# Running the shared expert's half units beside the routing in the second expert stage

## The chip, the cores and the metric

The kernel runs on one core of one Trainium2 chip. Its time is the device time of one execution in microseconds (us); where several executions were timed, their median is given. TensorE (PE) multiplies matrices, VectorE (DVE) does elementwise work and reductions, ScalarE (ACT) the table functions, GpSimd (POOL) elementwise work beside them, and SyncE (SP) issues the DMAs. Each engine works off its own queue in order and waits on semaphores.

## The reference

Two blocks, each a gated cross-attention and a gated mixture of experts, over x of 4 x 256 x 256. The change concerns the second mixture of experts (all tokens, 64 routed experts of width 64, four per token, and two shared experts of width 256):

```python
xm = x.mean(axis=1)
h1 = gelu(xm @ te_W1.T + te_b1)
task_dist = softmax(h1 @ te_W2.T + te_b2)                 # dataset head
dom = task_dist @ affinity.T                              # one row per batch
logits = (flat @ Wr.T).reshape(b, t, E) + 0.5 * dom[:, None, :]
scores = softmax(logits)
_, topk_idx = top_k(logits + router_bias, K)              # K = 4
topk_scores = scores[topk_idx] / (sum + 1e-8)
combine = zeros(n, E); combine[topk_idx] += topk_scores   # the shares
h = silu(flat @ Wg[e]) * (flat @ Wu[e])                   # for every expert
out = sum_e (h * combine[:, e]) @ Wd[e]
out = out + sum_i (silu(flat @ Sg[i]) * (flat @ Su[i])) @ Sd[i]   # shared
```

The shared experts take no shares: they need the tokens alone. flat is the layernorm of x, 1024 tokens.

## The kernel before

The program has four stages in one order: attention, experts, attention, experts. Between them the tokens are normalized and turned (`act_turn`, `pe_turn`, `norm`), so that xnT holds them with features on the partitions.

In an expert stage the work is cut into units of 128 hidden columns: in the second stage four units of the shared experts (128 columns each) and then 32 pairs of routed experts. A unit is done in two half units of 512 tokens each. A half unit is `pe_up` (L377: six matmuls for the gate into bank 4, six for the up product into bank 5), ScalarE's silu and VectorE's product (`act_ffn` L319, `ffn` L1545), and `pe_down` (L394: six matmuls, added into banks 0 to 3, which `pe_zero` L368 has cleared by four matmuls with zeros). All products are of split numbers: a high and a low part, three matmuls for one. ScalarE copies the high part of the hidden values (L333), VectorE subtracts it for the low one (L1561). POOL splits the weights of a unit (`split_weights` L667: L674, L675 for gate and up, L679, L680 for down) and makes the low part of the tokens (`stream_rest` L662). TensorE's order is up of half unit j+1, then down of half unit j. Weights and shares have two slots each. For a routed half unit VectorE first multiplies the silu with the experts' shares (L1553), which SP has broadcast to the partitions (wB) from a scratch tensor (w1s) in DRAM.

The second expert stage runs in this order before:

- SP (from L531): router constants, `shared` weights 0 to 3, then `store_shares` (waits for the turned shares, stores them, waits for the landing), then `pair1` for the routed pairs, which loads weights and broadcasts shares.
- TensorE (L1164 to L1211): the turn; the dataset head (two products, one small transpose); then, for each of eight token tiles, two products with the router's weights and one with the affinities; eight transposes of the shares; `pe_zero`; then the half units.
- VectorE (L1687 to L1728): mean of the tokens, the softmax of the dataset head, `shifted` (copy of the logits, maximum, subtract), exp on ScalarE, bias, four largest of 64 (max and match-replace over eight tiles), normalizing, `keep_shares` (L1540), and then `ffn` for the eight half units of the shared experts, and the loop over routed pairs.
- ScalarE (L858 to L868): gelu and exp of the dataset head, exp of the router, then silu and copies of the half units.

So the shared half units stand behind the whole routing in all queues.

Of the kernel before, what the change touches and what calls it, by code (L numbers as in the profile page):

```python
# [31 lines left out]
P = 128  # L32
# [121 lines left out]
def program(nc, a, out, stages=4):  # L154

    ctx = ExitStack()
    with ctx:
# [3 lines left out]
        def sb(name, shape, dt=F32, scope=ctx):  # L161
# [131 lines left out]
            "logits_made r_shifted r_exp sel_ready pos_made w_ready w_turned wT_ready "  # L293
# [25 lines left out]
        def act_ffn(act, u0, i, units, q0):  # L319

            for j in range(units):
# [131 lines left out]
        def _(sp):  # L453
# [138 lines left out]
            def pair1(e, slot, split, free):  # L592
# [3 lines left out]
                for j in range(2):  # L596
# [3 lines left out]
                    sp.dma_start(wd[n, slot, :], a["L1_ffn_Wd"][e * 2 + j]).then_inc(w, 16)  # L600
                w = s.bslot1 if slot else s.bslot0
# [4 lines left out]
            for j in range(2 * NSH):  # L606
                shared(j, j % 2, None if j < 2 else U0 + j - 1)
            store_shares(w1s, E1, 2)
            for r in range(2):
                pair1(r, r, U0 + 2 * NSH + r - 1, 2 * U0)  # L610
            with sp.Fori(1, E1 // 4) as i:
                for slot in range(2):
                    pair1(i * 2 + slot, slot, i * 2 + (U0 + 2 * NSH + slot - 1), i * 4 + (2 * U0 + 2 * slot - 2))
# [5 lines left out]
        def _(pool):  # L619
# [42 lines left out]
            def stream_rest(k):  # L662

                pool.wait_ge(s.xT_hi, KD * k)
                g_.tensor_tensor(xT[:, 1], xnT[:], xT[:, 0].bitcast(F32), ALU.subtract).then_inc(s.xT_lo, 1)
# [55 lines left out]
        def _(act):  # L721
# [67 lines left out]
            with act.Fori(0, U0 // 2) as i:  # L789
                act_ffn(act, 0, i, 4, 0)  # L790
# [71 lines left out]
            nc.scalar.activation(td[:, 1, :], td[:, 0, :], ACT.Exp).then_inc(s.tl_exp, 1)  # L862
            act.wait_ge(s.r_shifted, 2)
            nc.scalar.activation(re[:], rl[:, :, 0:E1], ACT.Exp).then_inc(s.r_exp, 1)
            u0 = 2 * U0
            act_ffn(act, u0, None, 8, None)
            with act.Fori(0, E1 // 4) as i:
                act_ffn(act, u0 + 8, i, 4, u0)  # L868
# [3 lines left out]
        def _(pe):  # L872
# [165 lines left out]
            pe.wait_ge(s.xT_lo, 1)  # L1038
# [127 lines left out]
            pe.wait_ge(s.router_loaded, 16 * 16)  # L1166
            pe.wait_ge(s.xm_ready, 1)
# [5 lines left out]
            pe.wait_ge(s.td_ready, 1)  # L1173
            nc.tensor.transpose(ps[0:ND, 6, 0:B], td[:, 3, :], ident[0:B, 0:B]).then_inc(s.td_turned, 1)
            pe.wait_ge(s.tdT_ready, 1)
            for t in range(NT):
                for k in range(KD):
                    nc.tensor.matmul(ps[:, 7, t * E1:(t + 1) * E1], xnT[:, k, t * P:(t + 1) * P], wr1[:, k, :],
                                     start=k == 0, stop=False)
                ins = nc.tensor.matmul(ps[:, 7, t * E1:(t + 1) * E1], tdT[:, t // TB, :], aff1[:], start=False, stop=True)  # L1180
            ins.then_inc(s.logits_made, 1)
            pe.wait_ge(s.w_ready, 2)
            for t in range(NT):
                ins = nc.tensor.transpose(ps[0:E1, 4 + t // 4, (t % 4) * P:(t % 4 + 1) * P], rw[:, t, :], ident[:])
            ins.then_inc(s.w_turned, 1)
            pe.wait_ge(s.wT_ready, 2)
# [3 lines left out]
            pe.wait_ge(s.xT_lo, 2)  # L1190
            pe_up(pe, u0, None, 0, U0 + 1)
            for j in range(8):
                if j < 7:
                    pe_up(pe, u0, None, j + 1, U0 + (j + 1) // 2 + 1)
                else:
                    pe_up(pe, u0 + 8, None, 0, first + 1)
                pe_down(pe, u0, None, j, U0 + j // 2 + 1)
            last = E1 // 4 - 1
# [17 lines left out]
        def _(dve):  # L1216
# [323 lines left out]
            def keep_shares(E, k):  # L1540

                dve.wait_ge(s.w_turned, k)
                v.tensor_copy(wtf[0:E, :], ps[0:E, 4:6, :].rearrange("p a n -> p (a n)")).then_inc(s.wT_ready, 1)

            def ffn(u0, i, units, q0):  # L1545
                for j in range(units):
# [40 lines left out]
            keep_shares(E0, 1)  # L1587
# [204 lines left out]
```

## Time and profile before

| what | value |
|---|---|
| median of three runs | 2046.72 us (2046.35 to 2048.01) |
| profiled execution, its own time | 2044.75 us |
| its span in the profile | 2043.0 us |
| TensorE busy | 1876.8 us (92%) |
| VectorE busy | 1173.6 us (57%) |
| ScalarE busy | 1037.8 us (51%) |
| POOL busy | 321.4 us (16%) |
| DMA | 96.56 MB, mean 47 GB/s |

The span is the time between the first and the last instruction that the profiler saw; the 1.75 us between it and the execution's own time lie around it. TensorE's share is an average over four stages, so a change within one stage is read there: by the stretches of that stage, by the chain of waits (which work ended last and released the next) and by the timeline of each engine. A busy TensorE is not one at its peak: the granted clock has two levels, 1.2 and 2.4 GHz, shown as 0.50 and 1.00.

### The profile page before, as it was taken

Reading aid. Unit: us, or ns where it says so; the run is one execution under the profiler, and the core shown is the slowest. Engines: PE = TensorE matmul, PEld = TensorE weight load, DVE = VectorE, ACT = ScalarE, POOL = GpSimd, SP = SyncE. Lnnn points to the kernel's source line nnn. Section 1 sums busy time; section 2 is a strip of 40 time slices with the busy share of each in tenths; the row PEclk is TensorE's granted clock in tenths of the full one; section 3 lists DMA queues with packets and bytes.
Section 4 is the critical chain, followed back from the end, with each engine's and each line's share of the span. In section 5 each row is a group of like instructions: output and inputs, shape, how many; then the busy total and the mean of one; then the engine's idle time right before and its main releaser. Section 6 shows DMA issues by size and latency. Waiting matters only on the chain.

```text
span 2043.0 us, 29167 instructions
## 1 busy us (share of the span) xinstructions
PE 1876.8 (92%) x8775; PEld 1281.9 (63%) x8775; DVE 1173.6 (57%) x1893; ACT 1037.8 (51%) x1703; POOL 321.4 (16%) x292
## 2 busy tenths in 40 slices
PE   5889898859997999999999999999999994999998
PEld 3444444548886666666666666666666663888886
DVE  8565746246666665546654476544665445566665
ACT  2576677613333565556655565555655551222222
POOL 3010101024441100000000000000000002444452
PEclk8899999969998999999999999999999995999999
DMA  2422404064441110000100001000000001255453
GB/s 90 101 59 59 99 19 101 1 215 109 108 114 40 33 33 0 0 0 1 33 0 0 0 1 33 0 0 0 0 1 0 0 0 36 73 116 112 108 115 78
DMA packets 110124, 96.56 MB, mean 47 GB/s; under 512 B 72836, under 2 KB 94472, under 8 KB 109416
## 3 DMA queue, kind: packets, MB, share of 16 engines
q1 hardware_dynamic: 110056, 95.67, 18.8%
q8 instruction: 41, 0.67, 0.1%
q14 instruction: 27, 0.22, 0.0%
HBM read 73.73 MB, written 1.44 MB: 37 GB/s over the span
## 4 chain that ended last, share of the span: by engine, by line
PE 81%; DVE 10%; ACT 2%; SPq 2%; POOL 2%; issue 2%; DMA 1%; ACTq 0%; DVEq 0%; POOLq 0%
PE ps L1137 18%; PE ps L1074 17%; PE ps L390 16%; PE ps L401 8%; PE ps L954 4%; PE ps L941 4%; PE ps L1151 3%; PE ps L1085 2%; PE ps L888 2%; DVE s_rk L1631 2%; SPq L491 2%; POOL s_stage L705 1%; PE ps L1109 1%; PE ps L1146 1%; DVE s_rq L1627 1%
## 5 line engine op out<-in xcount | busy, mean ns | idle before, releaser
L852 ACT ACTIVATE s_p<-ps,s_g,s_rk 128x256 f32<-128x256 f32 (+1 forms) x832 | 416.7, 560 | 298.5 <-PE ps L1074 268.5
L1074 PE MATMUL ps<-s_qq,s_ctxT 128*128 (+2 forms) x1248 | 498.9, 513 | 2.7 <-ACT s_ksq L826 2.7
L1137 PE MATMUL ps<-s_p,s_ctx 128*128 128x512 f32 (+1 forms) x832 | 416.7, 595 | 12.8 <-ACT s_p L852 12.8
L1663 DVE TENSOR_TENSOR s_dsum<-s_dsum,s_p 128x512 f32<-128x512 f32 (+1 forms) x384 | 265.8, 692 | 234.0 <-ACT s_p L852 222.3
L1074 PEld LDWEIGHTS ps<-s_qq,s_ctxT 128*128 128x128 f32 (+1 forms) x1248 | 231.3, 186 | 200.0 <-issue 163.3
L390 PE MATMUL ps<-s_xT,s_wgus 128*128 128x512 f32 x1440 | 350.4, 393 | 3.8 <-DVE s_hw L1559 3.5
L390 PEld LDWEIGHTS ps<-s_xT,s_wgus 128*128 128x128 f32 x1440 | 272.6, 189 | 62.4 <-DVE s_hw L1559 3.9
L770 ACT ACTIVATE s_p<-ps,s_bsm 128x1024 f32<-128x1024 f32 x208 | 219.3, 1110 | 93.1 <-PE ps L954 82.9
L1137 PEld LDWEIGHTS ps<-s_p,s_ctx 128*128 128x128 f32 (+1 forms) x832 | 156.9, 189 | 76.8 <-ACT s_p L852 24.6
L1561 DVE TENSOR_TENSOR s_hs<-s_hw,s_hs 128x512 fp32r<-128x512 f32 x120 | 141.3, 1177 | 82.5 <-ACT s_hs L333 82.5
L401 PE MATMUL ps<-s_hs,s_wds 128*128 128x512 f32 x720 | 183.9, 391 | 1.8 <-DVE s_hs L1561 1.8
L333 ACT CAST s_hs<-s_hw 128x512 fp32r<-128x512 f32 x120 | 74.5, 621 | 196.0 <-DVE s_hw L1559 196.0
L941 PE MATMUL ps<-s_qz,s_kT 96*128 96x512 f32 x416 | 155.6, 473 | 16.6 <-ACT s_p L770 8.6
L1074 PE MATMUL ps<-s_wk,s_ctxT 128*128 128x512 f32 (+1 forms) x624 | 167.8, 413 | 2.4 <-ACT s_ksq L826 2.2
L401 PEld LDWEIGHTS ps<-s_hs,s_wds 128*128 128x128 f32 x720 | 135.0, 189 | 31.7 <-DVE s_hs L1561 2.7
L705 POOL TENSOR_TENSOR s_stage<-s_stage,s_rq 128x2048 f32<-128x2048 f32 x8 | 28.9, 3611 | 784.5 <-DVE s_rq L1635 784.5
L826 ACT ACTIVATE s_ksq<-ps 128x512 f32<-128x512 f32 (+1 forms) x208 | 117.7, 607 | 67.5 <-PE ps L1074 39.2
L1631 DVE TENSOR_REDUCE s_rk<-s_ksq 128x4 f32<-128x512 f32 (+1 forms) x208 | 130.9, 676 | 33.6 <-ACT s_ksq L826 33.1
L329 ACT ACTIVATE s_sg<-ps 128x512 f32<-128x512 f32 x120 | 71.8, 598 | 132.1 <-PE ps L390 131.9
L1074 PEld LDWEIGHTS ps<-s_wk,s_ctxT 128*128 128x128 f32 (+1 forms) x624 | 111.1, 184 | 38.9 <-issue 9.8
L1553 DVE TENSOR_TENSOR s_hh<-s_sg,s_wB 128x512 f32<-128x512 f32 x112 | 77.4, 691 | 92.8 <-ACT s_sg L329 82.5
L941 PEld LDWEIGHTS ps<-s_qz,s_kT 96*128 96x128 f32 x416 | 70.2, 194 | 83.0 <-issue 55.1
(240 smaller groups left out, 1837.2 us busy)
## 6 DMA issues: line engine op xcount, KB each, us to landing
s_wB<-w1s SPq DMA_DIRECT2D x64, 256.0 KB, 3.9
s_kT<-s_kst SPq DMA_DIRECT2D x96, 128.0 KB, 2.3
s_kT<-s_kst SPq DMA_DIRECT2D x96, 80.0 KB, 2.1
s_wB<-w0s SPq DMA_DIRECT2D x16, 384.0 KB, 3.7
s_wB<-w0s SPq DMA_DIRECT2D x16, 256.0 KB, 4.1
s_wgu<-in_L_ffn_Wg_dram SPq DMA_DIRECT2D x64, 64.0 KB, 2.8
s_wgu<-in_L_ffn_Wu_dram SPq DMA_DIRECT2D x64, 64.0 KB, 2.6
s_wd<-in_L_ffn_Wd_dram SPq DMA_DIRECT2D x64, 64.0 KB, 2.5
```

Of the source, the lines that this page charges most:

```text
L390: ins = nc.tensor.matmul(ps[:, 4 + g, :], wgus[:, slot, w, g, k, :], xT[:, x_, k, n], start=c == 0, stop=c == len(ops) - 1)
L401: ins = nc.tensor.matmul(ps[:, 2 * half + k, :], wds[:, slot, w, k * P:(k + 1) * P], hs[:, j % 2, h, :], start=False, stop=False, skip_gro ...
L770: nc.scalar.activation(p0[:, n % 4, :], ps[:, 2 * (n % 3):2 * (n % 3) + 2, :].rearrange("p a n -> p (a n)"), ACT.Exp, bias=bsm[:, col:col ...
L826: nc.scalar.activation(ksq1[0:r, n % KSQ, :], ps[0:r, n % 4, :], ACT.Square).then_inc(s.k1_squared, 1)
L852: ins = nc.scalar.activation(p1[0:r, BANK1[t], j, :], ps[0:r, BANK1[t], j * SQ:(j + 1) * SQ], ACT.Exp, bias=g1[0:r, 3:4], scale=rk_col(t, ...
L941: ins = nc.tensor.matmul(ps[:, 2 * (n % 3) + i, :], kT0[0:32 * COPIES, g, i, t * P:(t + 1) * P], qz[0:32 * COPIES, g % 2, i, :], start=Tru ...
L954: ins = nc.tensor.matmul(ps[32 * h:32 * h + 32, SUMBANK, dca * SQ:dca * SQ + SQ], vg[:, b % 2, t + dca, c:c + 2 * D0], p0[:, n % 4, h * SQ ...
L1074: ins = nc.tensor.matmul(out, lhs(x_), rhs(y_), start=first and n == 0, stop=last and n == 2)
L1137: nc.tensor.matmul(ps[:, 4, :], ctx1[0:ROWS1[t], t, :], p1[0:ROWS1[t], BANK1[t], :, :].rearrange("p a n -> p (a n)"), start=t == 0, stop=t ...
L1561: v.tensor_tensor(hs[:, j % 2, 1, :], hw[:, j % 2, :], hs[:, j % 2, 0, :].bitcast(F32), ALU.subtract).then_inc(s.hs_lo, 1)
L1631: v.tensor_reduce(rk1[0:r, u, 4 * q:4 * q + 4], ksq1[0:r, n % KSQ, :].rearrange("p (h d) -> p h d", h=4), AX, ALU.add).then_inc(s.k1_reduc ...
L1663: v.tensor_tensor(dsum[0:r, :], dsum[0:r, :], pt[0:r, :], ALU.add).then_inc(s.summed, 1)
```

## The change

- TensorE multiplies the tokens with the router's weights right behind the turn, into bank 7, without the affinity part. The dataset head follows, then the zeroing and the shared half units. The transpose of the dataset distribution stands behind up(1), four products with the affinities (one per batch, into bank 6) behind down(0), and the transposes of the shares (into banks 6 and 7, no longer 4 and 5) behind down(4).
- VectorE adds the affinities to its copy of the logits in an instruction of its own. Its routing work is put between the half units 0 to 5 of the shared experts.
- ScalarE does silu and copies of half units 0 to 2, then the router's exp, then 3 to 7.
- POOL makes the low part of the tokens in two instructions, one for each half of the tokens (in the first expert stage as well, since both use the same function). TensorE waits for the first half before up(0), and for the second before up(1).
- SP loads the weights of the first two routed pairs ahead of the store of the shares. `pair1` is split into `pair1` (weights) and `shares1` (broadcasts).

The diff, without the lines that only pass a range where a count stood, or a bank number:

```diff
-            def pair1(e, slot, split, free):
+            def pair1(e, slot, split):
 
                 sp.wait_ge(s.wd_split, split)
...
+
+            def shares1(e, slot, free):
...
                 w = s.bslot1 if slot else s.bslot0
                 sp.wait_ge(s.h1_made, primed(free))
                 for j in range(2):
@@ -605,12 +608,15 @@
 
...
             for j in range(2 * NSH):
                 shared(j, j % 2, None if j < 2 else U0 + j - 1)
+            for r in range(2):
+                pair1(r, r, U0 + 2 * NSH + r - 1)
             store_shares(w1s, E1, 2)
             for r in range(2):
-                pair1(r, r, U0 + 2 * NSH + r - 1, 2 * U0)
+                shares1(r, r, 2 * U0)
             with sp.Fori(1, E1 // 4) as i:
                 for slot in range(2):
-                    pair1(i * 2 + slot, slot, i * 2 + (U0 + 2 * NSH + slot - 1), i * 4 + (2 * U0 + 2 * slot - 2))
+                    pair1(i * 2 + slot, slot, i * 2 + (U0 + 2 * NSH + slot - 1))
+                    shares1(i * 2 + slot, slot, i * 4 + (2 * U0 + 2 * slot - 2))
 
             store(sp)
...
             def stream_rest(k):
 
                 pool.wait_ge(s.xT_hi, KD * k)
-                g_.tensor_tensor(xT[:, 1], xnT[:], xT[:, 0].bitcast(F32), ALU.subtract).then_inc(s.xT_lo, 1)
+                for half in range(2):
+                    n = slice(half * HALF, (half + 1) * HALF)
+                    g_.tensor_tensor(xT[:, 1, :, n], xnT[:, :, n], xT[:, 0, :, n].bitcast(F32), ALU.subtract).then_inc(s.xT_lo, 1)
...
             nc.scalar.activation(td[:, 1, :], td[:, 0, :], ACT.Exp).then_inc(s.tl_exp, 1)
+            u0 = 2 * U0
+            act_ffn(act, u0, None, range(3), None)
             act.wait_ge(s.r_shifted, 2)
             nc.scalar.activation(re[:], rl[:, :, 0:E1], ACT.Exp).then_inc(s.r_exp, 1)
-            u0 = 2 * U0
-            act_ffn(act, u0, None, 8, None)
+            act_ffn(act, u0, None, range(3, 8), None)
...
-            pe.wait_ge(s.xT_lo, 1)
+            pe.wait_ge(s.xT_lo, 2)
...
             pe_turn(pe, 3)
             pe.wait_ge(s.router_loaded, 16 * 16)
+            for t in range(NT):
+                for k in range(KD):
+                    ins = nc.tensor.matmul(ps[:, 7, t * E1:(t + 1) * E1], xnT[:, k, t * P:(t + 1) * P], wr1[:, k, :],
+                                           start=k == 0, stop=k == KD - 1)
+            ins.then_inc(s.logits_made, 1)
...
             pe.wait_ge(s.xm_ready, 1)
...
             pe.wait_ge(s.te_gelu, 1)
             nc.tensor.matmul(ps[0:B, 6, 0:ND], h1t[:], te2[:], start=True, stop=True).then_inc(s.tl_made, 1)
-            pe.wait_ge(s.td_ready, 1)
-            nc.tensor.transpose(ps[0:ND, 6, 0:B], td[:, 3, :], ident[0:B, 0:B]).then_inc(s.td_turned, 1)
-            pe.wait_ge(s.tdT_ready, 1)
-            for t in range(NT):
-                for k in range(KD):
-                    nc.tensor.matmul(ps[:, 7, t * E1:(t + 1) * E1], xnT[:, k, t * P:(t + 1) * P], wr1[:, k, :],
-                                     start=k == 0, stop=False)
-                ins = nc.tensor.matmul(ps[:, 7, t * E1:(t + 1) * E1], tdT[:, t // TB, :], aff1[:], start=False, stop=True)
-            ins.then_inc(s.logits_made, 1)
-            pe.wait_ge(s.w_ready, 2)
-            for t in range(NT):
-                ins = nc.tensor.transpose(ps[0:E1, 4 + t // 4, (t % 4) * P:(t % 4 + 1) * P], rw[:, t, :], ident[:])
-            ins.then_inc(s.w_turned, 1)
-            pe.wait_ge(s.wT_ready, 2)
             pe_zero(pe)
             u0, first = 2 * U0, U0 + 2 * NSH
 
-            pe.wait_ge(s.xT_lo, 2)
+            def turn_dataset():
+
+                pe.wait_ge(s.td_ready, 1)
+                nc.tensor.transpose(ps[0:ND, 6, 0:B], td[:, 3, :], ident[0:B, 0:B]).then_inc(s.td_turned, 1)
+
+            def affinities():
+
+                pe.wait_ge(s.tdT_ready, 1)
+                for b in range(B):
+                    ins = nc.tensor.matmul(ps[:, 6, b * E1:(b + 1) * E1], tdT[:, b, :], aff1[:], start=True, stop=True)
+                ins.then_inc(s.aff_made, 1)
+
+            def turn_shares():
+
+                pe.wait_ge(s.w_ready, 2)
+                for t in range(NT):
+                    ins = nc.tensor.transpose(ps[0:E1, 6 + t // 4, (t % 4) * P:(t % 4 + 1) * P], rw[:, t, :], ident[:])
+                ins.then_inc(s.w_turned, 1)
+
+            pe.wait_ge(s.xT_lo, 3)
             pe_up(pe, u0, None, 0, U0 + 1)
+            pe.wait_ge(s.xT_lo, 4)
             for j in range(8):
                 if j < 7:
                     pe_up(pe, u0, None, j + 1, U0 + (j + 1) // 2 + 1)
                 else:
                     pe_up(pe, u0 + 8, None, 0, first + 1)
+                if j == 0:
+                    turn_dataset()
                 pe_down(pe, u0, None, j, U0 + j // 2 + 1)
+                if j == 0:
+                    affinities()
+                if j == 4:
+                    turn_shares()
             last = E1 // 4 - 1
...
-            def keep_shares(E, k):
+            def keep_shares(E, k, bank):
 
                 dve.wait_ge(s.w_turned, k)
-                v.tensor_copy(wtf[0:E, :], ps[0:E, 4:6, :].rearrange("p a n -> p (a n)")).then_inc(s.wT_ready, 1)
-
...
+            def ffn(u0, i, halves, q0):
+                for j in halves:
...
+            u0 = 2 * U0
+            ffn(u0, None, (0,), None)
             dve.wait_ge(s.td_turned, 1)
             v.tensor_copy(tdT[:], bc(ps[0:ND, 6, 0:B], P)).then_inc(s.tdT_ready, 1)
-            shifted(E1, 2)
+            dve.wait_ge(s.logits_made, 2)
+            me.do(v.tensor_copy(rr[:, :, 0:E1], ps[:, 7, :].rearrange("p (t e) -> p t e", t=NT)))
+            ffn(u0, None, (1,), None)
+            dve.wait_ge(s.aff_made, 1)
+            me.do(v.tensor_tensor(rr[:, :, 0:E1].rearrange("p (b t) e -> p b t e", t=TB), rr[:, :, 0:E1].rearrange("p (b t) e -> p b t e", t=TB),
+                                  ps[:, 6, 0:B * E1].rearrange("p (b e) -> p b e", b=B).unsqueeze(2).to_broadcast([P, B, TB, E1]), ALU.add))
+            me.do(v.tensor_reduce(rsm[:, 0, :], rr[:, :, 0:E1], AX, ALU.max))
+            v.tensor_tensor(rl[:, :, 0:E1], rr[:, :, 0:E1], bc(rsm[:, 0, :], E1), ALU.subtract).then_inc(s.r_shifted, 1)
+            ffn(u0, None, (2,), None)
+            dve.wait_ge(s.r_exp, 2)
             me.did(v.tensor_reduce(rsm[:, 3, :], re[:], AX, ALU.add))
...
             me.do(v.memset(m8[:, :, TOP1:TOPS], -FAR))
+            ffn(u0, None, (3,), None)
             for t in range(NT):
                 me.did(v.match_replace(rr[:, t, :], m8[:, t, :], rl[:, t, :], FAR))
             me.wait()
             me.do(v.tensor_scalar(rr[:, :, 0:E1], rr[:, :, 0:E1], 0.5 * FAR, None, ALU.is_gt))
+            ffn(u0, None, (4,), None)
             me.do(v.tensor_tensor(rw[:], re[:], rr[:, :, 0:E1], ALU.mult))
             me.do(v.tensor_reduce(rsm[:, 1, :], rw[:], AX, ALU.add))
             me.do(v.scalar_tensor_tensor(out=rsm[:, 2, :], in0=rsm[:, 3, :], scalar=1e-8, in1=rsm[:, 1, :],
                                          op0=ALU.mult, op1=ALU.add))
             me.do(v.reciprocal(rsm[:, 4, :], rsm[:, 2, :]))
             v.tensor_tensor(rw[:], rw[:], bc(rsm[:, 4, :], E1), ALU.mult).then_inc(s.w_ready, 1)
-            keep_shares(E1, 2)
-            u0 = 2 * U0
-            ffn(u0, None, 8, None)
+            ffn(u0, None, (5,), None)
+            keep_shares(E1, 2, 6)
+            ffn(u0, None, (6, 7), None)
             with dve.Fori(0, E1 // 4) as i:
-                ffn(u0 + 8, i, 4, u0)
```


## Rows read from the trace of the kernel before

**Rows 1.** Stretches (start:end in us; PEclk granted clock, 1.00 is 2.4 GHz).

```profile
core 0: us, PE busy (x) PEld busy (x) DVE busy (x) ACT busy (x) POOL busy (x), PEclk, DMA share, GB/s
1700.50:1736.40 35.90, 16.61 (x63) 13.74 (x63) 16.80 (x47) 6.03 (x8) 10.48 (x8) 0.50 0.08 22
1709.00:1722.80 13.80, 13.29 (x48) 11.40 (x48) 0.46 (x1) 0.00 (x0) 2.14 (x3) 0.50 0.09 29
1772.40:2020.00 247.60, 247.60 (x1094) 205.00 (x1094) 155.97 (x183) 73.87 (x121) 121.22 (x122) 1.00 0.49 110
443.00:446.50 3.50, 3.50 (x11) 2.44 (x9) 0.00 (x0) 1.62 (x2) 0.00 (x0) 0.64 0.34 102
```

**Rows 2.** Chain of waits, 1684 to 1760: start, us, engine, tile, line, count.

```profile
1699.81 0.70 DVE s_xnT L1247
...
1703.23 1.00 PE ps L1169 x4
...
1711.24 1.04 PE ps L1178 x4
1712.29 0.61 PE ps L1180 x2
...
1733.21 1.93 PE ps L1184 x8
1735.16 1.23 DVE s_wtf L1543
1736.43 1.89 PE ps L371 x4
1738.32 5.95 PE ps L390 x24
1744.27 1.36 PE ps L401 x6
1745.63 2.72 PE ps L390 x12
```

**Rows 3.** Timeline around the routing and the first half units.

```profile
1703.01 4.49 POOL L665 TENSOR_TENSOR s_xT<-s_xnT,s_xT 128x2048 fp32r<-128x2048 f32 x1
...
1704.57 0.20 PE L1172 MATMUL ps<-s_te,s_h1t 128*4 128x4 f32 x2 [0.36 <-ACT s_h1t L860]
...
1743.01 0.69 DVE L1561 TENSOR_TENSOR s_hs<-s_hw,s_hs 128x512 fp32r<-128x512 f32 x1 [0.69 <-ACT s_hs L333]
...
1745.53 1.29 POOL L675 TENSOR_TENSOR s_wgus<-s_wgu,s_wgus 128x512 fp32r<-128x512 f32 x1
1745.74 1.63 DVE L1561 TENSOR_TENSOR s_hs<-s_hw,s_hs 128x512 fp32r<-128x512 f32 x1 [0.69 <-ACT s_hs L333]
```

**Rows 4.** Timeline of TensorE, start of the first expert stage.

```profile
441.59 4.94 PE L390 MATMUL ps<-s_xT,s_wgus 128*128 128x512 f32 x12
```

**Rows 5.** Timeline of ScalarE, in the first expert stage's loop.

```profile
564.52 1.28 ACT L329 ACT_TABLE_LOAD   x1 [1.44 <-PE ps L390]
565.82 0.60 ACT L329 ACTIVATE s_sg<-ps 128x512 f32<-128x512 f32 x1
```

**Rows 6.** VectorE alone, routing in three stretches: busy us (instructions).

```profile
1725.70:1728.38 2.68, 2.52 (x12) 0.50 0.00 0
1728.38:1730.56 2.18, 2.10 (x17) 0.50 0.00 0
1730.56:1733.18 2.62, 2.44 (x5) 0.50 0.00 0
```

**Rows 7.** Timeline of TensorE at the end.

```profile
2037.25 1.09 PE L411 MATMUL ps<-s_ident,s_wB 128*128 128x128 f32 x8 [2.51 <-DVE s_wB L1732]
```

**Rows 8.** DMA issues, 1690 to 1790: count, KB each, median us to landing.

```profile
s_wB<-w1s SPq DMA_DIRECT2D x8, 256.0 KB, 3.9
...
w1s<-s_wtf SPq DMA_DIRECT2D x1, 256.0 KB, 3.0
```

**Rows 9.** Timeline of VectorE, first routed product of the first expert stage.

```profile
450.50 0.69 DVE L1553 TENSOR_TENSOR s_hh<-s_sg,s_wB 128x512 f32<-128x512 f32 x1 [10.30 <-DMA s_wB<-w0s]
```

More of the change, by code:

```diff
@@ L292, in program @@
             "ctx_made cx_turned cxT_act y0_made x_updated "
-            "logits_made r_shifted r_exp sel_ready pos_made w_ready w_turned wT_ready "
+            "logits_made aff_made r_shifted r_exp sel_ready pos_made w_ready w_turned wT_ready "
             "xm_ready te_made te_gelu tl_made tl_shifted tl_exp td_ready td_turned tdT_ready "
@@ L317, in act_split, with act_ffn @@
                 nc.scalar.copy(xT[:, 0, j, :], xnT[:, j, :]).then_inc(s.xT_hi, 1)
-        def act_ffn(act, u0, i, units, q0):
-            for j in range(units):
+        def act_ffn(act, u0, i, halves, q0):
+            for j in halves:
                 act.wait_ge(s.g_made, at(u0, i, 4, j + 1))
@@ L789, in _ @@
             with act.Fori(0, U0 // 2) as i:
-                act_ffn(act, 0, i, 4, 0)
+                act_ffn(act, 0, i, range(4), 0)
             if stages < 3:
@@ L862, in _ @@
             nc.scalar.activation(td[:, 1, :], td[:, 0, :], ACT.Exp).then_inc(s.tl_exp, 1)
+            u0 = 2 * U0
+            act_ffn(act, u0, None, range(3), None)
             act.wait_ge(s.r_shifted, 2)
             nc.scalar.activation(re[:], rl[:, :, 0:E1], ACT.Exp).then_inc(s.r_exp, 1)
-            u0 = 2 * U0
-            act_ffn(act, u0, None, 8, None)
+            act_ffn(act, u0, None, range(3, 8), None)
             with act.Fori(0, E1 // 4) as i:
-                act_ffn(act, u0 + 8, i, 4, u0)
+                act_ffn(act, u0 + 8, i, range(4), u0)
         @block.tensor
@@ L1538, in shifted @@
                 dve.wait_ge(s.r_exp, k)
-            def keep_shares(E, k):
+            def keep_shares(E, k, bank):
                 dve.wait_ge(s.w_turned, k)
-                v.tensor_copy(wtf[0:E, :], ps[0:E, 4:6, :].rearrange("p a n -> p (a n)")).then_inc(s.wT_ready, 1)
-            def ffn(u0, i, units, q0):
-                for j in range(units):
+                v.tensor_copy(wtf[0:E, :], ps[0:E, bank:bank + 2, :].rearrange("p a n -> p (a n)")).then_inc(s.wT_ready, 1)
+            def ffn(u0, i, halves, q0):
+                for j in halves:
                     n = slice((j % 2) * HALF, (j % 2 + 1) * HALF)
@@ L1586, in _ @@
                                    in1=wf, op0=ALU.is_lt, op1=ALU.mult).then_inc(s.w_ready, 1)
-            keep_shares(E0, 1)
+            keep_shares(E0, 1, 4)
             with dve.Fori(0, U0 // 2) as i:
-                ffn(0, i, 4, 0)
+                ffn(0, i, range(4), 0)
             for half in range(2):
@@ L1723, in _ @@
             v.tensor_tensor(rw[:], rw[:], bc(rsm[:, 4, :], E1), ALU.mult).then_inc(s.w_ready, 1)
-            keep_shares(E1, 2)
-            u0 = 2 * U0
-            ffn(u0, None, 8, None)
+            ffn(u0, None, (5,), None)
+            keep_shares(E1, 2, 6)
+            ffn(u0, None, (6, 7), None)
             with dve.Fori(0, E1 // 4) as i:
-                ffn(u0 + 8, i, 4, u0)
+                ffn(u0 + 8, i, range(4), u0)
             for half in range(2):
```

## The prediction

> **What bounds the kernel now.** I read the stretches first. From 1772.4 to 2020 us TensorE is busy all the time at a granted clock of 1.00 (the 2.4 GHz level); from 1700.5 to 1736.4 it is busy 16.61 of 35.9 us at 0.50 (1.2 GHz) [rows 1]. So the expert stage has a full part, which the change leaves alone, and a routing part, in which the engines take turns. The chain of waits shows the turns [rows 2]: the turned tokens are kept by 1700.51, the dataset head's first product starts at 1703.23, eight rounds of logits and affinity of 1.65 us follow (the second and its affinity at 1711.24 and 1712.29 stand for them), VectorE then selects, the shares are turned from 1733.21 (1.93 us) and kept (1.23), the banks are zeroed (1.89), and the 24 matmuls of the first two half units begin at 1738.32. From there a half unit costs 2.72 us (up) and 1.36 (down), 4.08 in all, and TensorE never rests. Nothing of the shared expert needs the shares, so the idle time ahead of 1738.32 is what can be had.
>
> **When the first half unit can start.** The logits now come first, without the affinity part. A round was 1.04 us of token products and 0.61 of affinity [rows 2]; eight rounds of 1.05 from 1700.6 end at 1709.0. The dataset head, queued behind them on TensorE, starts at 1709.0 and not at 1703.23, 5.8 us later. Its second product came 1.34 us after the first (1704.57 against 1703.23) [rows 2, 3], so 1710.35, and the zeroing, which no longer waits for the shares, follows at 1710.55 and ends 1.89 later. The first half unit starts at 1712.45: **25.9 us earlier** than 1738.32. Weights of the first unit are there. The low part of the tokens, one POOL instruction of 4.49 us from 1703.01, was complete at 1707.5 [rows 3]; in two halves it ends a little later than that, the first near 1705.3, and either is ahead of 1712.45. So this edit is worth nothing, hidden by logits and dataset head; without that cover the first half would give 2.2 us. In the first expert stage the same split only adds an instruction on POOL in a stretch where TensorE waits for shares; I take 0, bounds -0.5 and +0.5.
>
> **The clock's ramp.** Before, the first 24 matmuls took 5.95 us, where two half units at full clock take 2 x 2.72 = 5.44 [rows 2]: 0.5 us of ramp. In the first expert stage twelve such matmuls from 441.59 took 4.94 us and the clock was 0.64 in 443 to 446.5 [rows 1, 4]: 2.2 over 2.72. I take the same 0.5 as before; the ends are 0.5 better and 1.7 worse.
>
> **What is put among the half units.** Times are for the changed kernel, half units 0 to 7, each engine followed in its own order; up and down of the steady pace are 2.72 and 1.36 us [rows 2], so up(1) ends at 1718.4 and down(0) at 1719.8. Per half unit VectorE does a product (0.69), waits 0.69 for ScalarE's copy, and subtracts (0.69, or 1.63 where POOL's 1.29 us split runs) [rows 3]. Without a visitor it needs 2.1 to 3.0 of 4.08 us, and a half unit may run some 1.5 us late before TensorE notices, since its result is wanted one half unit later.
> - Half unit 0: copy of the dataset distribution (0.69) and of the logits (0.69). TensorE computes four affinities behind down(0), where there were eight: 0.61 each at half clock [rows 2], 0.3 if it scales with the clock: 1.2 us, all of it in TensorE's queue. Ends 0.9 and 2.4. Up(2) starts at 1721.0, 1.2 behind an undisturbed pace.
> - Half unit 1: add, maximum, subtract, three ops of 0.69: shifted logits at 1724.5. Product 2 at 1724.55 instead of 1723.9, its subtraction done at 1727.1 after a POOL op; down(2) was due at 1727.75, so nothing is lost.
> - Half unit 2: ScalarE loads the exp table (1.28), does the exp (about 0.6, as the silu of the same size), loads silu's again (1.28) [rows 5]: free of its copy at 1725.9, exp done 1727.8, silu(3) done 1729.7. VectorE waits for the exp, then has 2.68 us of sum, bias and eight maxima [rows 6], 0.4 more behind a POOL split: product 3 from 1731.0 to 1731.7, 3 us late. TensorE wants silu(3) at 1729.1, product 3 at 1731.15 and its subtraction (1733.1) straight behind: it loses 0.7 and 0.65 us.
> - Half unit 3: match-replace and compare, 2.18 us [rows 6]. Product 4 ends at 1736.05, wanted at 1735.85: 0.25 us. All losses of this kind: 1.7 us; ends 0 and 4.5.
> - Half unit 4: product, sums, reciprocal and scaling, 2.62 us [rows 6]. Down(4) ends at 1738.8, the weights of the routing at 1740.1 if POOL is not met, at 1741.2 if the two products of two SBUF tensors are held up beside it as the subtraction is [rows 3]. TensorE stands at the wait for them, with up(6) queued behind: 1.9 us; ends 0 and 3.5. Then eight transposes: 1.92 us at half clock, 1.09 at full [rows 7]; I take 1.1, since they took that even after 2.5 us of idling.
> - Half unit 5: shares kept (1.23 [rows 2]) behind its subtraction, near 1744.5, since product 5 stood behind the weights and ends at 1741.9, copy and subtraction follow. Up(6) runs meanwhile, and the pace is TensorE's again.
>
> **Sum.** 25.9 - 1.2 - 1.7 - 1.9 - 1.1 = **20.0 us less**. Two things could eat into it later. SP now issues the loads of the first two routed pairs ahead of the store of the shares; they wait for POOL's splits, which follow down(1) and down(3) (1726.5 and 1736.0 by the walk), and are out by 1739.3, ahead of the shares at 1744.5, so the order costs nothing. The store lands in 3.0 us, each of the two broadcasts in 3.9 [rows 8]: 1744.5 + 3.0 + 3.9, and 0.8 for SP to issue three of them (my estimate; the far bound is in the second rival), is 1752.2. The first routed half unit wants them at 1753.0 (up(6) plus two paces of 4.08 and the matmuls and silu of its own). The slack is 0.8 us. The loop after it and the output are the same.
>
> **Two rules of the Trainium skill.** VectorE's subtraction takes 0.69 us alone and 1.63 beside a POOL op of 1.29, ending 0.55 behind it [rows 3]. The Trainium skill (SBUF — State Buffer, section Who interferes with whom) makes this an exclusive lock for VectorE ops with two SBUF inputs or in a two-port mode. By that rule the bias add, the two products of half unit 4 and the compare can be blocked too, and the routing, which had POOL to itself before, now meets its splits: the sum would be some 19.4 by the rule and 20.5 if only the subtraction were subject to it.
> A table load of 1.28 us at 564.52 is followed by its silu at 565.82, with nothing between [rows 5]. The Trainium skill (ScalarE: Activation LUTs, section What ACT_TABLE_LOAD costs) puts some 1.4 us of draining on top of each load. By that rule silu(3) would be 2.8 us later, product 3 some 1.5, and the sum 18.5: this speaks against the change and is the fourth rival; the row speaks against the rule.
>
> **Rivals.**
> - VectorE falls behind in every half unit: most of the routing ops with two SBUF inputs meet a POOL op of up to 1.29 us, the 1.7 becomes 4.5 and the 1.9 becomes 3.5: 15.6 us gained, 2031.1.
> - The broadcasts of the shares are late. In the first expert stage VectorE stood 10.30 us for them after its copy [rows 9], among heavy weight traffic. From 1744.5 that is 1754.8 against 1753.0: 1.8 us lost, 2028.6. Here the queue is empty, which speaks against it.
> - Everything fits: the slack of 1.5 us hides VectorE, the weights come at 1740.1 or earlier, affinities 0.9: 22.5 us gained, 2024.2. For it: VectorE is busy 156 of 247.6 us in the loop [rows 1].
> - The extra cost at the table loads: 1.5 us, 2028.2.
> - Slower: the clock. TensorE was busy 13.29 of 13.8 us during logits and stayed at 0.50 [rows 1]; only after the zero writes and wide matmuls did it rise. With waits and narrow products between the half units it could stay at 1.2 GHz, or fall back: twelve in 4.94 us are 0.41 each [rows 4], so a half unit of 18 takes 7.4 us instead of 4.08. From 20 / 3.3 = 6 slow half units on the gain is gone; with all eight, 26.6 us are lost, and the kernel is 6.6 slower, 2053.4. Against it: the 512-column matmuls came with a rise of the clock within 5 us of their start both times [rows 2, 4], and 2.51 us of idling at the end left the transposes fast [rows 7].
> - It does not do what it says, because the compiled order still puts a wait ahead of the half units, or the end is not set by TensorE: no change. TensorE is busy 247.60 of 247.60 us behind [rows 1], which leaves little room.
>
> **How the numbers follow.** The profiled run took 2044.75 us, its span 2043.0 and 1.75 around it; the change leaves the 1.75 alone. Less 20.0 that is 2024.8. The median of the three runs is 2046.72, 2.0 above the profiled one, so the median of the changed kernel is 2026.7; with the terms unrounded (19.9) it is 2026.8, which I give. Chances: forecast 0.55 (its own range 2024.9 to 2028.9), VectorE behind 0.16, late broadcasts 0.08, tables 0.03, all fits 0.13, slow clock 0.03, no change 0.02. The range reaches over the better case and over the first rival, with a little of the medians' spread of 1.7: 2023.2 to 2031.6; left out are the slow clock, no change and the tails of two rivals. A measurement of this kernel can tell about 0.2%, 4 us. Faster 0.95, within 0.2% 0.02, slower 0.03.
>
> **What the profile would show.** Right: eight rounds of logits from 1700.6 to 1709, zero writes near 1710.5, up matmuls from 1712.5 at clock 1.00 soon after; two further table loads; TensorE idle before the transposes of the shares for 1 to 2.5 us; up(6) near 1742; no wait of the first routed product on a DMA; last up group of the kernel 20 us earlier. Wrong: a clock of 0.50 behind 1716; VectorE idle times before its products gone in half units 5 to 7; the gap of 1.9 larger, or a wait for the broadcast. It would also be wrong if the affinity or transposes cost the same as at half clock.

## The result and the profile after

| | before | after |
|---|---|---|
| median, first comparison | 2046.53 us (4 executions) | 2024.62 us (2021.41 to 2027.91) |
| ratio of the times | | 0.9871, 95% interval 0.9846 to 0.9896 |
| profiled execution, its own time | 2044.75 us | 2027.91 us |
| its span | 2043.0 us | 2025.8 us |

By the medians the gain is 21.9 us, by the ratio 26.4 (21.3 to 31.5); the quotient of the two medians, 0.9893, lies inside the ratio's interval. The stages ahead of the change ended 5.4 us later in this trace than in that of before, so the two are compared from the point at which the turned tokens are kept: 1700.50 us before, 1705.88 after. The first routed product of VectorE (the share broadcast is used there for the first time) comes 71.95 us later before and 49.26 after: **22.7 us less**, against the 20.0 of the sum. From there to the end it is 270.6 us in both.

The chain of waits of the kernel after (start, us, engine, tile, line, count), the longer pieces:

```profile
1705.98 7.06 PE ps L1178 x32
...
1714.67 1.49 PE ps L371 x3
1716.16 5.93 PE ps L390 x24
...
1722.18 1.60 PE ps L401 x6
1723.78 1.03 PE ps L1199 x8
1724.81 2.98 PE ps L390 x12
...
1729.23 1.28 ACT L874
...
1732.55 1.11 DVE s_m L1748 x8
...
1735.94 1.60 DVE s_rr L1753 x8
...
1741.89 1.60 DVE s_rw L1762
1743.54 1.06 PE ps L1206 x8
1744.61 2.75 PE ps L390 x12
1747.35 1.36 PE ps L401 x6
```

The logits are one piece of 7.06 us, without the affinities between them; the first up matmuls start 10.3 us behind the kept tokens, where they started 37.8 us behind them before [rows 2]. TensorE is the chain up to down(1); from there to the transposes the chain runs over ScalarE's exp table and VectorE's visitors, and it comes back to TensorE at 1743.54. Behind 1744.61 the pace is 2.72 and 1.36 again, as in [rows 2].

Stretches of the kernel after (PE busy, PEld, DVE, ACT, POOL busy with counts, granted clock, DMA share, GB/s): logits, first up matmuls, the wait for the shares, the routed part.

```profile
1705.90:1713.00 7.10, 7.02 (x33) 7.05 (x34) 4.49 (x2) 2.34 (x3) 7.02 (x6) 0.50 0.18 55
1716.10:1722.00 5.90, 5.90 (x25) 4.54 (x23) 1.79 (x3) 2.59 (x4) 0.40 (x1) 0.93 0.23 68
1740.00:1744.40 4.40, 2.74 (x17) 1.91 (x15) 3.94 (x7) 0.28 (x1) 2.35 (x2) 1.00 0.36 89
1755.10:2010.00 254.90, 254.90 (x1126) 211.06 (x1125) 159.66 (x188) 76.42 (x125) 122.30 (x122) 1.00 0.49 108
```

TensorE is full in the last, as before [rows 1], and idle 1.66 of 4.4 us in the third. The timeline there shows why the wait ends when it does:

```profile
1741.68 1.26 POOL L683 TENSOR_TENSOR s_wgus<-s_wgu,s_wgus 128x512 fp32r<-128x512 f32 x1
1741.89 1.59 DVE L1762 TENSOR_TENSOR s_rw<-s_rw,s_rsm 128x512 f32<-128x512 f32 x1
...
1743.54 1.06 PE L1206 MATMUL ps<-s_ident,s_rw 128*64 128x128 f32 x8 [1.66 <-DVE s_rw L1762]
```

VectorE's last product takes 1.59 us instead of 0.69, and ends 0.54 us behind POOL's split: the pattern of the subtraction in [rows 3].

### The profile page after: what moved, and what is told of

It is laid out like the page before. It is cut to its first block, busy times and chain, and to the rows that moved or that the text cites. A ratio compares the mean times of both kernels' runs of the same rounds, so it can differ in the third digit from the quotient of the medians.

```text
span 2025.8 us, 29157 instructions
## 1 busy us (share of the span) xinstructions
PE 1876.0 (93%) x8765; PEld 1280.9 (63%) x8767; DVE 1171.5 (58%) x1894; ACT 1042.1 (51%) x1705; POOL 322.7 (16%) x294
## 4 chain that ended last, share of the span: by engine, by line
PE 80%; DVE 10%; SPq 2%; ACT 2%; issue 2%; POOL 2%; DMA 1%; ACTq 0%; DVEq 0%; POOLq 0%
PE ps L1146 18%; PE ps L1083 17%; PE ps L390 16%; PE ps L401 8%; PE ps L963 4%; PE ps L950 4%; PE ps L1160 3%; PE ps L1094 3%; SPq L491 2%; DVE s_rk L1657 2%; PE ps L897 2%; POOL s_stage L713 1%; PE ps L1118 1%; PE ps L1155 1%; DVE s_rq L1653 1%
## 5 line engine op out<-in xcount | busy, mean ns | idle before, releaser
L1587 DVE TENSOR_TENSOR s_hs<-s_hw,s_hs 128x512 fp32r<-128x512 f32 x120 | 137.1, 1143 | 82.6 <-ACT s_hs L333 82.6
L329 ACT ACTIVATE s_sg<-ps 128x512 f32<-128x512 f32 x120 | 71.9, 599 | 116.4 <-PE ps L390 116.3
```

Of the source, the lines that this page charges most:

```text
L1587: v.tensor_tensor(hs[:, j % 2, 1, :], hw[:, j % 2, :], hs[:, j % 2, 0, :].bitcast(F32), ALU.subtract).then_inc(s.hs_lo, 1)
```

## The experiments

All stretches are given from the kept tokens to the first routed product ("the stretch"). Before it is 71.95; the rest of the program is 1968 to 1978 us in all profiles.

**The changed kernel again, and the kernel before.** No edit.

> The changed kernel again, in more rounds. Theory A: the gain is made in the second expert stage alone, 22.7 us between the kept tokens and the first routed product (71.95 us before, 49.26 after), and the rest of the 6.5 us between its runs is where TensorE's granted clock falls in the second attention stage: near 2046.5 - 22.7 = 2023.8, that stretch 49.3 us again within 1. Rival B: the change also moves something else, and the true gain is 26 or more: below 2021, with other stretches shorter.

> The kernel before, unchanged, profiled again: how much of the spread between executions lies outside the changed stretch. Theory A: from kept tokens to first routed product 71.95 us again, within 0.5; what differs between executions is the number of spells at half clock in the second attention stage (three of them there before, six in both profiles of the changed kernel), some 0.4 us per us of half clock. Rival B: the stretch itself varies in the kernel before too.

> The kernel before once more, for the spread between executions. Theory A: 71.9 to 72.1 from kept tokens to first routed product; the rest of the program 1970 to 1977 us.

> The changed kernel once more. Theory A: the stretch is 49.3 where the logits run at half clock and 47.0 where they run at full clock; the rest of the program 1970 to 1977 us, so the kernel's own gain is 22.7 to 25.0 and anything above in a comparison of times is the spread of the rest. Rival: another value of the stretch, below 46.

> The changed kernel beside it on the same chip: 24 to 27 us below the kernel before in the median of many executions, of which 22.5 to 25 in the changed stretch; the executions of either spread by 8 us or more with their mean granted clock, some 12 us for each 0.01 of it.

| run | ratio to before (95%) | median, us | stretch, us |
|---|---|---|---|
| after_again | 0.9866 (0.9845 to 0.9887) | 2024.61 against 2050.87 | 47.03 |
| after_third | one execution | 2026.99 | 49.54 |
| after_fourth | 0.9882 (0.9865 to 0.9898) | 2026.54 against 2051.44 | 49.35 |
| before_again | 0.9999 (0.9983 to 1.0015) | 2049.69 against 2050.38 | 72.06 |
| before_third | one execution | 2042.27 | 72.26 |

The runs with a single execution (before_third, after_third, and below sp_order, warm_before, head_first, one_low, pool_late) are read by their stretches alone.

The stretch of before is 71.95 to 72.26 in three profiles; the changed kernel's is 49.3 to 49.5 in three and 47.0 in one, outside what after_again was expected to show (49.3 within 1). What is different in after_again stands in two stretches of it, logits and first up matmuls:

```profile
1704.80:1708.60 3.80, 3.74 (x32) 3.65 (x32) 3.72 (x2) 2.32 (x3) 3.72 (x4) 1.00 0.05 15
1711.70:1718.80 7.10, 7.10 (x26) 5.38 (x25) 2.11 (x6) 3.31 (x6) 3.63 (x5) 0.77 0.19 57
```

The same 32 instructions take 3.74 us at clock 1.00, where they took 7.02 at 0.50. 3.3 us are won there, 1.1 given back: the clock falls again behind the small products and zero writes that follow, and the 24 up matmuls take 7.07 us instead of 5.93. So the changed stretch has more than one length, and the kernel's own gain there is 22.4 to 25.2 us.

The rest of the gain is spread. Over the 51 executions of before whose mean granted clock is at hand, the time runs from 2042.3 to 2060.8 us, median 2050.4, and follows the clock: 2043.9 at 0.966, 2060.8 at 0.954, about 12 us for 0.01 (correlation -0.87). The 14 of the changed kernel run from 2020.1 to 2030.1, median 2026.0. The medians differ by 24.4 us, which lies within what the stretch gives.

The profiled executions alone would say less: outside the stretch they took 1968.2 to 1971.1 us in the three of before and 1975.3 to 1977.8 in the four of the changed kernel (before_third lies outside what it was expected to show in both, 72.26 against 71.9 to 72.1 and 1968.2 against 1970 to 1977). That this is the change's doing is unlikely, since runs with most or all of its edits lie at both ends (warm_both 1968.7, both 1969.5, pool_late 1970.8, both_pool_late 1978.0) and logits_only, which has neither the overlap nor the split low part, is at 1976.3. Theory A of before_again held for the stretch, within 0.5. Its reason for the rest, the number of spells at half clock in the second attention stage, failed: there were three in each profile of before, and six, six, three and three in those of the changed kernel, whose remainder was as long with three (1975.4 and 1977.8) as with six (1976.5 and 1975.3). Why the three profiled executions of before (2044.75, 2044.38, 2042.27) all lie at its short end was not settled.

**The logits' part alone, in the kernel before.**

```diff
+            for t in range(NT):
+                for k in range(KD):
+                    ins = nc.tensor.matmul(ps[:, 7, t * E1:(t + 1) * E1], xnT[:, k, t * P:(t + 1) * P], wr1[:, k, :], ...)
             pe.wait_ge(s.xm_ready, 1)
...
+            for b in range(B):
+                ins = nc.tensor.matmul(ps[:, 6, b * E1:(b + 1) * E1], tdT[:, b, :], aff1[:], start=True, stop=True)
```

> The kernel before with one part of the change alone: logits first, affinities as four products of their own and an add on VectorE; the half units stay behind the whole routing. Theory A: eight rounds without the affinities between them take 7.06 us and not 13.3, the dataset head starts 4.5 us later; the copy of the logits' maximum comes near 14.1 us behind the kept tokens instead of 23.1: 9 us faster, near 2037.5. Rival: the gain is all overlap and the rewrite is worth 8 affinities of 0.61, less the four and the add: 2 us or less, 2044.5.

Ratio 0.9954 (0.9938 to 0.9971), median 2041.61 against 2050.87: 9.3 us. The stretch is 62.27, 9.7 less. In this profile the logits ran at full clock, and the up matmuls behind the routing met a low one:

```profile
1705.40:1709.20 3.80, 3.74 (x34) 3.77 (x34) 2.61 (x2) 2.33 (x3) 3.71 (x4) 1.00 0.02 6
1732.00:1739.50 7.50, 7.50 (x26) 5.95 (x25) 1.38 (x2) 1.81 (x3) 0.00 (x0) 0.73 0.07 15
```

So theory A: the rival's 2 us are far off. The 9.7 of this profile are not free of the clock, which gave 3.3 us at the logits and took 1.5 in the up matmuls (7.42 and not 5.95); the interval of the ratio alone says 6 to 13 us. Splitting the products by kind and doing the logits while VectorE makes the mean is worth some 9 us alone; by subtraction the half units beside the routing bring the other 13 to 15.

**The order of head and logits undone, in the changed kernel** (the loop over the logits put behind the head's second product).

> The changed kernel with the order of logits and dataset head undone: the head's two products at 2.7 and 4.1 us behind the kept tokens, then the logits, then the zeroing. Theory A: up(0) starts when the logits' 7.06 us, begun at 4.3 and not at 0.1, and the zeroing are over: near 13 instead of 10.3, and everything behind it 2.5 us later: stretch 51 to 52 at half clock. Rival: the dataset head's softmax on VectorE set the pace, it is now 4 us earlier, and the stretch is 48 to 49.5.

Stretch 51.98, 2.6 over 49.35, with up(0) at 13.1 us behind the kept tokens and not 10.3. Theory A. TensorE's queue decides up to the start of the half units, not the head's softmax.

**The low part in one instruction.**

```diff
-                for half in range(2):
-                    n = slice(half * HALF, (half + 1) * HALF)
-                    g_.tensor_tensor(xT[:, 1, :, n], xnT[:, :, n], xT[:, 0, :, n].bitcast(F32), ALU.subtract).then_inc(s.xT_lo, 1)
+                g_.tensor_tensor(xT[:, 1], xnT[:], xT[:, 0].bitcast(F32), ALU.subtract).then_inc(s.xT_lo, 1)
```

> The changed kernel with the low part of the tokens in one instruction again. Both theories of the clock: complete near 7.0 us behind the kept tokens, up(0) starts at 10.3 (or 6.9 where the clock is high during the logits): no difference, 49.3 or 47.0 to 47.5. Rival: the split is part of the gain: 2 us longer.

```profile
1703.62 7.06 PE ps L1176 x32
...
1713.80 7.10 PE ps L390 x24
```

Up(0) starts 10.28 us behind the kept tokens (1703.52), to the hundredth as in after. The stretch is 50.45, but the 1.1 us more are in the 24 matmuls (7.10 and not 5.93 to 6.20): the clock rose 3.4 us behind the start of up(0) and not 0.8 to 1.4. It had fallen 6.8 us ahead of the kept tokens (some 9 in the three profiles of the changed kernel with slow logits), before POOL's instruction ran, so nothing ties this to the split. Worth nothing here, as forecast.

**SP's order undone.**

```diff
+            store_shares(w1s, E1, 2)
             for r in range(2):
                 pair1(r, r, U0 + 2 * NSH + r - 1)
-            store_shares(w1s, E1, 2)
-            for r in range(2):
                 shares1(r, r, 2 * U0)
```

> The changed kernel with SP's order undone: store of the shares ahead of the weights of the first two routed pairs. Theory A: the weights of the first routed pair are then issued 3 us behind the store (near 49 us after the kept tokens minus 5) and split after that, and its broadcasts come 2.6 us later: TensorE waits 3 to 5 us before the first routed half units, 49.3 becomes 51.5 to 54. Rival: the loads had time enough, 49.3 as before.

The chain of waits from the transposes on:

```profile
1738.34 1.06 PE ps L1205 x8
1739.40 2.00 PE ps L390 x9
1741.42 3.00 DMA w1s<-s_wtf
1744.44 0.37 SPq L599
...
1747.04 2.06 DMA s_wd<-in_L_ffn_Wd_dram
...
1749.28 1.03 POOL s_wgus L681
...
1750.38 1.27 POOL s_wgus L682
1751.70 5.19 PE ps L390 x12
```

Here the logits ran at full clock, and VectorE's last product missed POOL's split (0.70 us): the transposes began 33.1 us behind the kept tokens, 4.5 earlier than in after. The first routed product then comes 17.3 us behind them instead of 11.6 (11.6 in after_again too, whose logits were fast as well), since store, loads and split stand one behind the other and TensorE waits. 5.7 us are lost; part of that is the clock, which falls during the wait (5.19 us for 12 matmuls and not 2.72). The stretch of 50.41 alone would have hidden most of it. Theory A, above its 3 to 5 us: SP's order is part of the gain.

**POOL's split behind the routing.**

```diff
+            pool.wait_ge(s.w_ready, 2)
             with pool.Fori(0, E1 // 4) as i:
```

> The changed kernel, with POOL waiting for the finished weights of the routing before it splits the first routed pair's weights. Theory A (VectorE's last product of two SBUF tensors, 1.59 us beside POOL's split, is held up by it): that product takes 0.70 us, TensorE's wait ahead of the transposes is 0.8 us and not 1.7, the stretch 48.4 at half clock and 46.1 at full; the split, 2 us later, has slack. Rival: the product is long for another reason, 1.6 again; or the later split makes TensorE wait: 49.3 or more.

```profile
1736.46 0.69 DVE L1763 TENSOR_TENSOR s_rw<-s_rw,s_rsm 128x512 f32<-128x512 f32 x1
...
1737.21 1.07 PE L1207 MATMUL ps<-s_ident,s_rw 128*64 128x128 f32 x8 [0.76 <-DVE s_rw L1763]
```

0.69 instead of 1.59 us, TensorE's wait 0.76 instead of 1.66, the stretch 48.59 with the logits at half clock (49.3 to 49.5 in the changed kernel). Theory A: the collision costs 0.9 us on the path, and the split had room to come later.

**Two more moves on TensorE, and all three.**

```diff
+            pe_zero(pe)
             pe.wait_ge(s.te_gelu, 1)
             nc.tensor.matmul(ps[0:B, 6, 0:ND], h1t[:], te2[:], start=True, stop=True).then_inc(s.tl_made, 1)
-            pe_zero(pe)
...
-                    pe_up(pe, u0, None, j + 1, U0 + (j + 1) // 2 + 1)
+                    pe_up(pe, u0, None, j + 1, U0 + (j + 1) // 2 + 1, turn_shares if j == 5 else None)
...
-                if j == 4:
-                    turn_shares()
```

(`pe_up` calls its last argument between the gate's matmuls and the others.)

> The changed kernel with two more moves on TensorE: the zeroing ahead of the dataset head's second product (hides the 1.3 us between the head's two products), and the transposes of the shares between gate and up of half unit 6 (hides the 1.66 us in which TensorE waits for the shares). Theory A (TensorE's queue sets the pace, each idle time on it counts): 2.3 us shorter than the changed kernel in the stretch from kept tokens to first routed product, 47.0. Rival (VectorE sets the pace in half units 3 to 6): at most 1 us shorter.

> The same wait together with the zeroing ahead of the dataset head's second product and the transposes of the shares inside up(6). Theory A: transposes near 36.8 us behind the kept tokens and not 37.8, last half units 1 us ahead of the kernel with two moves: 2.2 us ahead of the changed kernel in all, near 2022; the best version so far. Rival: the broadcasts of the shares are what TensorE then waits for, no gain over the two moves.

both: 0.9861 (0.9842 to 0.9881), median 2021.67 beside 2024.61 of the changed kernel. Stretch 48.93, and 1.0 less behind it. The zeroing let up(0) start 0.5 us earlier (9.77 and not 10.28), but it ended no earlier (16.27 and 16.21), since the clock rose no earlier; the transposes inside up(6) brought the 1.3. So neither expectation was right as it stood: 1.3 us and not 2.3, and the clock, not VectorE, took the rest. The first routed product now waits 1.59 us for its broadcast, in the slack that TensorE has.

both_pool_late: 0.9866 (0.9848 to 0.9883), median 2023.89 beside 2026.54 of the changed kernel on the same chip. In its profile (kept tokens at 1707.98) the clock stayed high, and TensorE ran through the shares without a wait:

```profile
1708.00:1711.80 3.80, 3.72 (x34) 3.75 (x34) 2.84 (x2) 2.34 (x3) 3.64 (x5) 1.00 0.01 2
1717.90:1724.00 6.10, 6.10 (x29) 4.67 (x30) 3.58 (x6) 1.84 (x3) 3.67 (x5) 1.00 0.23 69
```

Stretch 44.57, which can't be set beside the 48.93 of both: logits and up matmuls ran at another clock. Both kernels are some 3 us below the changed one in the medians, with intervals that overlap; that either is faster than it, and which of the two is the better, was not settled.

**Filler ahead of the turn.**

```diff
+            for r in range(112):
+                nc.tensor.matmul(ps[:, 0, 0:P], onesb[:], onesb[:], start=True, stop=True)
             pe_turn(pe, 3)
```

> The changed kernel with 112 matmuls of ones (128 columns, into bank 0, read by nobody) in the 7.4 us in which TensorE waits for the normalized tokens. Theory A (what the logits and the start of the half units cost hangs on the clock that is granted when they begin, and that depends on the work right ahead of them): logits take 3.8 us and not 7.06 in every execution, the stretch from kept tokens to first routed product is 44.5 to 45.5 instead of 49.3 and 47.0. Rival: the clock falls in the turn anyway, or the filler delays it: 47 to 51.

> The same filler, with the zeroing ahead of the dataset head's second product and the transposes of the shares inside up(6). Theory A: 1.3 us less than warm by the transposes, the broadcasts of the shares just in time: 43 to 44.5. Rival: the first routed product now stands for its broadcast for over 2 us and the time is that of warm.

> The kernel before with the same filler. Theory A: behind the turn TensorE has 8 us with 1.4 us of work there, the clock falls before the logits or soon after they begin: 71.95 becomes 68 to 72. Rival: the high clock holds through the logits, their 13.4 us become 7, and the stretch is near 65: then a third of the gain was to be had without moving the half units.

The filler kept the clock at 1.00 through the turn in warm; then it fell behind the logits, and the up matmuls met it low:

```profile
1700.00:1705.40 5.40, 3.39 (x38) 2.74 (x35) 4.47 (x15) 1.83 (x4) 0.00 (x0) 1.00 0.35 86
1712.70:1720.50 7.80, 7.74 (x25) 5.95 (x25) 3.39 (x6) 3.29 (x5) 5.92 (x6) 0.73 0.10 32
```

warm: stretch 48.06, ratio 0.9879 (0.9857 to 0.9901), the same as without filler. Up(0) started at 7.3 us, released by the first half of the low part (POOL L673, 4.94 to 7.25): here the split did set the start. The second half of the low part followed 2.3 us later, which is an estimate of what one instruction would have cost; no run of the changed kernel has one instruction and fast logits. warm_both: 47.76, 0.9876 (0.9856 to 0.9897), outside both expectations: the clock fell within the logits, which took 4.82 us, and the first routed product waited 1.58 us for its broadcast.

warm_before: 75.18, 3.23 us over 71.95 and outside both expectations. The filler held the clock to 2.3 us behind the kept tokens, and the logits ran at 0.50 as in before. The clock accounts for 1.25 us: the up matmuls took 7.20 and not 5.95. The other 2.0 are VectorE beside POOL. A step of the dataset head's softmax on 4x4 values, which took 0.22 us in head_first, stood until POOL's low part of the tokens was done; first in before, where POOL's row is in [rows 3], then in warm_before:

```profile
1705.17 2.35 DVE L1698 TENSOR_SCALAR s_td<-s_td 4x4 f32<-4x4 f32 x1
```

```profile
1704.77 4.49 POOL L665 TENSOR_TENSOR s_xT<-s_xnT,s_xT 128x2048 fp32r<-128x2048 f32 x1
...
1705.55 3.73 DVE L1700 TENSOR_SCALAR s_td<-s_td 4x4 f32<-4x4 f32 x1
```

That is 1.4 us more; another 0.6 is the scaling of the mean, 0.78 and not 0.17, beside POOL's split of weights. So some 2 of the 71.95 us of before were this wait, ahead of its logits. In the changed kernel it took 0.40 in after, off the chain; with fast logits it was on the chain again (1.98 in both_pool_late, ahead of the first silu).

Theory A fell in its second half: a clock that is high at the logits need not stay so. It fell ahead of the up matmuls in after_again and warm and stayed high through them in sp_order and both_pool_late, with the same products between; what decides was not shown. The rival held for warm.

## Why the prediction was right or wrong

- **That the idle time goes, and that TensorE's queue sets the start: right** (head_first).
- **The start of the half units: 11.95 us behind the kept tokens forecast, 10.28 measured.** The failed term is the round of logits, 1.34 us too large in all. 1.05 us was read from a round with an affinity product behind it [rows 2]; without it, two token products take 7.06 / 8 = 0.88. The same kind of loop in the first expert stage, 32 instructions in 7.02 us in the trace of before, would have given it. The rest is the head, whose second product came 1.10 us behind the first and not 1.34, and 0.1 in the zeroing, 1.82 us (the 1.49 in the chain are three of its four matmuls).
- **The clock as a constant: wrong.** The forecast took half clock for the logits and allowed for the ramp only. In one of four profiles of the changed kernel the logits ran at full clock, worth 2.2 to 2.5 us net. The rival of a clock that stays low did not occur; the clock went the other way.
- **The ramp (0.5): right** at 5.93 against 5.95. Over all runs in which the 24 matmuls stand in one piece it was 5.82 to 7.72; the far end of the forecast, 5.95 plus 1.7, was just passed in warm.
- **Affinities (1.2) and transposes (1.1): right**, 1.03 and 1.06. A term that the sum left out: from up(1) to the affinities TensorE took 1.69 us for down(0) with the transpose of the dataset distribution, 0.33 over the 1.36 of a down.
- **VectorE among the half units (1.7): too large.** From the end of the affinities to the wait for the shares TensorE took 17.07 us for four half units (1724.81 to 1741.88), 0.75 over 4 x 4.08. The walk had product 3 at 30.5 us behind the kept tokens and it came at 28.0: 1.7 of that is the earlier start; the other 0.8 was not traced. The mechanism (the exp's two table loads, then the eight maxima) is in the chain.
- **The wait for the shares (1.9): right**, 1.66, with the collision that the Trainium skill's rule (SBUF — State Buffer, section Who interferes with whom) asks for; pool_late showed its price, 0.9 us. The first of the two products in this half unit started ahead of POOL's split (0.69 us), the second met it (1.59).
- **No draining behind a table load: right.** The exp of 0.63 us follows its load at once (1729.23 + 1.28 = 1730.51, exp at 1730.52), so the 1.4 us of the Trainium skill (ScalarE: Activation LUTs, section What ACT_TABLE_LOAD costs) do not appear here either.
- **The broadcasts in time: right**, the first product waited for ScalarE. The slack was nearer 0.4 us than 0.8, by an estimate: in both the broadcast was there 8.1 us behind the issue of the store (1740.65 to 1748.75); the same from 1746.62 in after is 1754.7, and the product began at 1755.14. With the transposes 1.3 us earlier in TensorE's order (both) it waited 1.59 us for the DMA, and TensorE did not.
- **The low part split: worth nothing, right** with slow logits; in warm, with fast ones, its first half set the start. In the first expert stage, forecast at 0, nothing is seen of it: from the copy of the shares to the first routed product 11.2 to 11.5 us in three profiles of before, 10.9 to 12.1 in four of the changed kernel, 11.0 in one_low.
- **The sum: 20.0 against 22.7 in the stretch, 2.7 too small.** The terms close it: 20.0, + 1.67 for the start, + 0.95 for VectorE, + 0.24 for the wait, + 0.23 for affinities, transposes and ramp, - 0.33 for the term left out, is 22.8.
- **Range and base: wrong.** The median of the first comparison, 2024.62, lies in the range; by the ratio the changed kernel is at 2020.1 us against a low end of 2023.2. Three executions within 1.7 us looked like a steady 2046.7, and the same kernel has a median of 2050.4 and a spread of 18.5 us over 51; the range took the spread of three numbers for that of the program. That the changed kernel's median over 14, 2026.0, is so near the 2026.8 forecast is luck: a base 3.7 us too low and a gain 4.5 too small offset each other.

## What to carry to other kernels

Work that needs no result of a serial stage goes beside it, and each visitor in a queue is costed by who stands behind it; here the longest one (2.6 us of VectorE behind ScalarE's exp) was larger than the 1.1 to 2.0 us that a half unit leaves free, and TensorE still lost only 0.75 us, since a half unit's result is wanted one half unit later. A duration is read from a row with the same neighbours: small products of one kind in a row were 16% cheaper than with another kind between them. Where the time follows the granted clock, a part is judged by its own stretch in two or more profiles, and the kernel by many executions.

## What the runs showed of the hardware

- The same 32 narrow fp32 instructions took 3.74 us at clock 1.00 and 7.02 at 0.50, in executions of one and the same kernel. Which of the two it was differed from execution to execution.
- A filler of 112 matmuls held the clock at 1.00 through the turn, and the time did not fall: the clock dropped in the narrow products behind it (warm, 0.73 over the up matmuls). In warm_before it fell ahead of the dataset head, and the logits ran at 0.50 as without filler.
- A VectorE instruction on 4x4 values took 2.35 us in before and 3.73 in warm_before, ending with POOL's 4.49 us subtraction over two SBUF tensors, and 0.22 in head_first. Size says nothing of what such a meeting costs on a serial chain.
- Work that starts earlier on a slow clock does not end earlier when the clock's rise does not move with it: 9.77 to 16.27 against 10.28 to 16.21 us (both, after).
